# First cross-attention of a two-layer decoder: context loaded in the stage before, chunks split beside the maxima, stacks filled from SBUF

## The reference

```python
def _L0_xattn_ref(q, k, v, mask, wq, bq, wk, bk, wv, bv, wo, bo):
    H, D_K = 16, 16                        # context k = v: 2 x 1024 x 256
    qh = _split_heads(q @ wq.T + bq, B)
    kh = _split_heads(k @ wk.T + bk, B)
    vh = _split_heads(v @ wv.T + bv, B)
    scores = jnp.einsum('bhqd,bhkd->bhqk', qh, kh) / math.sqrt(D_K)
    scores = jnp.where(mask == 0, jnp.float32(-1000000000.0), scores)
    out = jnp.einsum('bhqk,bhkd->bhqd', softmax(scores), vh)
    return out.transpose(0, 2, 1, 3).reshape(B, -1, D_MODEL) @ wo.T + bo
```

## Time and profile before

| what | us |
|---|---|
| median of 3 runs | 1187.73 |
| lowest, highest | 1184.6, 1197.11 |
| the profiled execution, its own time | 1187.39 |
| its span, first to last instruction | 1185.6 |
| first cross stage, first SP issue to the next stage's | 144.3 to 448.7 |
| its first score | 218.07 |
| hard cross stage, first instruction | 815.6 |

### The profile page before, as it was taken

The page is one execution under the profiler, slowest core; times in us unless marked ns, Lnnn a source line. Parts: engine busy times, 40 slices in busy tenths (PEclk is TensorE's granted clock), DMA queues, the critical chain, the costliest instruction groups (busy, mean ns, idle before and its releaser), DMA issues. The chain is left out here.

```text
span 1185.6 us, 13004 instructions
## 1 busy us (share of the span) xinstructions
PE 943.2 (80%) x4000; PEld 472.9 (40%) x4005; DVE 668.0 (56%) x1347; ACT 455.2 (38%) x900; POOL 307.0 (26%) x294
## 2 busy tenths in 40 slices
PE   6879677699999985996489999894958888636985
PEld 3435434123333245664345555453412223412554
DVE  5845585698999633121354445444667885323534
ACT  3775132067777740111143233321206666202321
POOL 7144654000000002001254444454210000065014
PEclk9989988589999996799699999997968999858998
DMA  6000047434535005112540000000321110342000
GB/s 197 1 1 1 18 143 187 115 89 120 151 104 165 6 1 199 50 61 63 205 180 1 1 1 1 1 0 23 73 48 46 39 40 1 137 157 83 27 9 27
DMA packets 45279, 82.13 MB, mean 69 GB/s; under 512 B 9881, under 2 KB 31433, under 8 KB 43273
## 3 DMA queue, kind: packets, MB, share of 16 engines
q1 hardware_dynamic: 42081, 75.55, 21.2%
q0 software_dynamic: 2176, 5.38, 1.3%
q10 hardware_dynamic: 960, 0.43, 0.1%
HBM read 60.08 MB, written 16.54 MB: 65 GB/s over the span
## 5 line engine op out<-in xcount | busy, mean ns | idle before, releaser
L1050 DVE TENSOR_REDUCE c_amx<-PS 128x1 f32<-128x512 f32 x256 | 158.4, 682 | 28.3 <-PE PS L961 28.0
L1141 ACT ACTIVATE c_aE<-PS 128x512 f32<-128x512 f32 x256 | 132.6, 603 | 44.8 <-PE PS L973 44.5
L1599 POOL TENSOR_SCALAR s_Pn<-s_Pr,s_rs 128x512 f32<-128x512 f32 x64 | 99.9, 1563 | 123.0 <-DVE s_rs L1626 122.8
L961 PE MATMUL PS<-c_aKs,c_aQs 99*128 99x512 bf16 x256 | 106.5, 419 | 19.5 <-DMA c_aQs<-c_q_stack 18.6
L67 POOL TENSOR_SCALAR rstd<-mv 128x4 f32<-128x4 f32 x10 | 2.3, 232 | 388.0 <-DVE mv L90 387.3
L1617 DVE TENSOR_REDUCE s_mx<-PS 128x1 f32<-128x512 f32 x64 | 44.2, 691 | 100.3 <-PE PS L1730 100.3
L973 PE MATMUL PS<-c_aQs,c_aKs 99*128 99x512 bf16 x256 | 95.8, 385 | 3.4 <-ACT c_aE L1141 2.3
L1683 ACT ACTIVATE s_Pr<-PS,s_nmx 128x512 f32<-128x512 f32 x64 | 44.0, 687 | 137.4 <-DVE s_nmx L1619 137.4
L1050 DVE TENSOR_REDUCE h_amx<-PS 128x1 f32<-128x512 f32 x128 | 79.8, 684 | 26.7 <-PE PS L961 26.5
L1748 PE MATMUL PS<-s_PT,s_V 128*128 128x512 f32 x128 | 67.1, 606 | 18.6 <-DVE s_PT L1633 18.2
L1141 ACT ACTIVATE h_aE<-PS 128x512 f32<-128x512 f32 x128 | 66.9, 603 | 33.5 <-PE PS L973 33.3
(11 more groups left out here) (372 smaller groups left out, 1718.2 us busy)
## 6 DMA issues: line engine op xcount, KB each, us to landing
area<-in_e_w SPq DMA_DIRECT2D x16, 512.0 KB, 9.1
area<-in_g_w SPq DMA_DIRECT2D x8, 1024.0 KB, 17.0
c_aVs<-c_VB SPq DMA_DIRECT2D x8, 512.0 KB, 16.5
g_B<-in_g_b SPq DMA_DIRECT2D x1, 4096.0 KB, 11.6
c_k_stack<-area SPq DMA_DIRECT2D x12, 256.0 KB, 4.6
c_aKs<-c_k_stack SPq DMA_DIRECT2D x8, 384.0 KB
area<-in_ctxT SPq DMA_DIRECT2D x2, 1024.0 KB, 10.0
c_q_stack<-area SPq DMA_DIRECT2D x16, 128.0 KB, 2.5
```

Source lines behind the costliest of these rows:

```text
L961: pe.matmul(PS[:, n % MB, :], self.Qs[u % 3][:, j, qt * P:(qt + 1) * P], self.Ks[u % 3][:, j % self.KH, half * BANK:(half + 1) * BANK], st ...
L1050: dve.tensor_reduce(self.mx[:, qt, j, half:half + 1], PS[:, n % MB, :], AX.X, ALU.max).then_inc(self.max_done, 1)
L1141: act.activation(self.E[kt % 2][:, j, :], PS[:, MB + x % XB, :], ACT.Exp, scale=0.25).then_inc(self.exp_done, 1)
L1599: pool.tensor_scalar(Pn[g % NPB][:, :], Pr[g % NPB][:, :], rs[:, g % NPB:g % NPB + 1], None, ALU.mult).then_inc(pn_ready, 1)
```

## The change

- **Early loads.** A new area `early` (8488 words a partition, released after the cross stage) holds mixer buffers and, once these are used up, key weights, context, mask, and the other small inputs of the cross stage (`EarlyKeys`). SP loads them in the mixer after the last gate tile has been read (ScalarE L642, the last of them started at 62.65 us). VectorE converts the mask in the mixer, before its last output. TensorE computes key chunks 0 and 1 at the mixer's end.
- **First unit first.** Only key chunks 0 and 1 and query chunk 0 (`near`) are split before the attention. VectorE makes their residuals and third parts. The other nine chunks (`far`), value tiles 0 to 7 and the product of value bias and output weights come beside the maxima of unit 0, in `prologue`, one chunk or two tiles after each group of four scores. Their first residual and third part are made by GpSimd, their first and second parts by ScalarE. Value tiles 8 to 15 come in units 0 to 3, two in each (`during`, kt = 3 on TensorE, kt = 4 on ScalarE).
- **Fill from SBUF.** The DRAM stacks of the cross stage go. SP fills each block of 16 rows of a stack by one DMA from 64 rows of a part (6 for keys, 6 for queries, of 128 and 64 KB), and two for the tails. Those of unit 0 are issued part by part as these become ready.
- **Values** are read by TensorE from VB directly, 17 columns wide instead of 32; no load into Vs, in both cross stages.
- **Value bias** goes through the output weights into the output bias instead of being added to each value tile.
- **Tails.** The query tail comes from DRAM as an input, in the hard stage also the key tail; GpSimd's operations for them go, in both stages. The key tail of the cross stage is made by ScalarE.
- **Expert weights** of the next stage are all loaded after the last unit's fill.

The diff, cut:

```diff
-AREA = 17160
+AREA = 16384
+EARLY = 8488
...
+    XC = [early.take([P, B, PAD + S]) for n in range(2)]
+    CV = [early.take([P, B, S]) for n in range(2)]
+    w_in = early.take([P, KD, 2 * DI + 2 * DS + HEADS])
+    keys = sh.keys
...
+            sp_.wait_ge(silu_ready, len(convs))
+            sp_.wait_ge(proj_taken, 2 * len(convs) + NT)
+            keys.load(sp_)
...
+            keys.mask_vector(dve)
...
+            pe.wait_ge(st_ready, states_before(NT))
+            pe.wait_ge(t1_ready, carried_before(NT))
+            keys.first_chunks(pe)
...
-VW = 32
+VW = HD + 1
+MW = 32
...
-                pe.wait_ge(self.v_loaded[u % 3], (u // 3 + 1) * 16)
+                self.wait_values(pe, u // NG)
                 if u > 0:
                     pe.wait_ge(self.o_copied, u)
             pe.wait_ge(self.exp_done, (u * KT + kt + 1) * GH)
             for j in range(GH):
-                last = pe.matmul(PS[32 * j:32 * j + 32, 6, :], self.Vs[u % 3][:, kt, j % self.KH, :],
+                last = pe.matmul(PS[32 * j:32 * j + VW, 6, :], self.V[:, u, kt, j % self.KH, :],
...
+                    if before_maxima:
+                        before_maxima(pe, u)
...
+                if during:
+                    during(pe, u, kt)
...
+            if prologue:
+                prologue(pe, c)
...
-        sp.dma_start(at.Vs[buf][:, :, :, :],
-                     values[:, bass.ds(u, 1), :, :, :].rearrange("p u t h c -> p (u t) h c")).then_inc(at.v_loaded[buf], 16)
...
+    RING = (6, 5, 3, 4, 7)
+    FIRST = 2
...
+    def load(self, sp):
+        A, NK = self.A, self.NK
+        sp.dma_start(self.wk[:, :, :], A["c_wk"]).then_inc(self.wk_in, 16)
+        sp.dma_start(self.ctxT[:, :, 0:NK], A["ctxT"][:, :, 0:NK]).then_inc(self.ctx_in[0], 16)
+        sp.dma_start(self.maski, A["mask"].unsqueeze(0).to_broadcast([P, B, NK])).then_inc(self.mask_in, 16)
+        for d, name in ((self.wq, "c_wq"), (self.wv, "c_wv"), (self.bq, "c_bq"), (self.bk, "c_bk"), (self.ktc, "c_ktc")):
+            sp.dma_start(d[tuple(slice(None) for _ in d.shape)], A[name]).then_inc(self.rest_in, 16)
+        sp.dma_start(self.ctxT[:, :, NK:2 * NK], A["ctxT"][:, :, NK:2 * NK]).then_inc(self.ctx_in[1], 16)
+    def mask_vector(self, dve):
+        dve.wait_ge(self.mask_in, 16)
+        dve.tensor_scalar(self.mask[:, :, :], self.maski, 0.0, None, ALU.not_equal).then_inc(self.masked, 1)
+    def chunk(self, pe, n, bank):
+        b, m, half = n // 4, n // 2 % 2, n % 2
+        c0 = b * self.NK + half * BANK
+        for k in range(KD):
+            last = pe.matmul(bank, self.wk[:, k, m * P:(m + 1) * P], self.ctxT[:, k, c0:c0 + BANK],
+                             start=(k == 0), stop=(k == KD - 1))
+        last.then_inc(self.mm, 1)
+    def first_chunks(self, pe):
+        pe.wait_ge(self.wk_in, 16)
+        pe.wait_ge(self.ctx_in[0], 16)
+        for n in range(self.FIRST):
+            self.chunk(pe, n, self.PS[:, self.RING[n], :])
+KEY_SLOTS = ((0, 3, 5), (1, 4), (2,))
+QUERY_SLOTS = ((0, 1, 2), (3, 4), (5,))
...
+    made = [("k", 0), ("k", 1), ("k", 2), ("k", 3), ("q", 0), ("k", 4), ("k", 5), ("q", 1), ("q", 2), ("k", 6), ("k", 7),
+            ("q", 3)] + [("v", t) for t in range(KT)] + [("bo", 0)]
+    taken_by_scalar = [("q", 1), ("q", 2), ("q", 3)] + [("v", t) for t in range(KT)] + [("bo", 0)]
+    taken_by_scalar += [("v", t) for t in range(KT, NV)]
+    near = [("k", 0), ("k", 1), ("q", 0)]
+    far = [("k", 2), ("k", 3), ("k", 4), ("k", 5), ("q", 1), ("q", 2), ("k", 6), ("k", 7), ("q", 3)]
...
+            def tails(u):
+                sp.dma_start(at.Qs[u % 3][TAIL:ROWS, :, :].rearrange("r h n -> r (h n)").bitcast(U16),
+                             A["q_tail"]).then_inc(at.loaded[u % 3], 16)
+                sp.wait_ge(tails_set, u // NG + 1)
+                sp.dma_start(at.Ks[u % 3][TAIL:ROWS, :, :], ktail[:, u // NG, :].unsqueeze(1)
+                             .to_broadcast([TAIL_ROWS, GH, NK])).then_inc(at.loaded[u % 3], 16)
+            def key_part(u, p):
+                b, g = divmod(u, NG)
+                src = KP[p][g % 2 * 64:g % 2 * 64 + 64, b, g // 2, :]
+                for slot in KEY_SLOTS[p]:
+                    sp.dma_start(at.Ks[u % 3][slot * HD:(slot + 1) * HD, :, :], src).then_inc(at.loaded[u % 3], 16)
+            def query_part(u, p):
+                b, g = divmod(u, NG)
+                src = QP[p][g % 2 * 64:g % 2 * 64 + 64, g // 2, b * S:(b + 1) * S]
+                for slot in QUERY_SLOTS[p]:
+                    sp.dma_start(at.Qs[u % 3][slot * HD:(slot + 1) * HD, :, :], src).then_inc(at.loaded[u % 3], 16)
+            def load(u, buf):
+                if u >= 2:
+                    pair = [("k", 2 * (u // 2)), ("k", 2 * (u // 2) + 1), ("q", u // 2)]
+                    sp.wait_ge(far_p2_ready, 1 + max(far.index(c) for c in pair))
+                    tails(u)
+                for p in range(3):
+                    if u == 0:
+                        sp.wait_ge((p0_ready, p1_ready, p2_ready)[p], 2)
+                    key_part(u, p)
+                    if u == 0:
+                        sp.wait_ge((p0_ready, p1_ready, p2_ready)[p], len(near))
+                    query_part(u, p)
+            for u in range(2):
+                tails(u)
             sp.dma_start(wo[:, :, :], A["c_wo"]).then_inc(wo_in, 16)
             sp.dma_start(bo[:, :], A["c_bo"]).then_inc(wo_in, 16)
+            sp.dma_start(bvc[:, :, :], A["c_bv"]).then_inc(wo_in, 16)
+            at.sync(sp, load, lambda: None)
+            for n in range(3):
+                sp.wait_ge(at.loaded[n], 16 * loads * len(range(n, UNITS, 3)))
+            sp.wait_ge(xb_ready, 1)
+            for e in range(ExpertWeights.EXP):
+                sh.weights[0].load_expert(sp, e)
...
+            pool.memset(VB[:, :, :, :, HD:VW], 1.0).then_inc(v_ones, 1)
+            def last_part(i):
+                pool.wait_ge(p1_ready, len(near) + i + 1)
+                pool.tensor_tensor(part(*far[i], 2), R[i % 4], part(*far[i], 1), ALU.subtract).then_inc(far_p2_ready, 1)
+            for i, c in enumerate(far):
+                pool.wait_ge(p0_ready, len(near) + i + 1)
+                if i >= 4:
+                    pool.wait_ge(far_p2_ready, i - 3)
+                pool.tensor_tensor(R[i % 4], F[i % 4], part(*c, 0), ALU.subtract).then_inc(far_r_ready, 1)
+                if i > 0:
+                    last_part(i - 1)
+            last_part(len(far) - 1)
...
+            normalise(0)
+            dve.wait_ge(keys.rest_in, 80)
+            for n in range(2):
+                take_keys(n, FK[n])
+            normalise(1)
+            for n in range(2):
+                dve.wait_ge(p0_ready, n + 1)
+                dve.tensor_tensor(RK[n], FK[n], part("k", n, 0), ALU.subtract).then_inc(r_ready, 1)
+            at.set_ones(dve)
+            dve.wait_ge(p0_ready, 3)
+            dve.scalar_tensor_tensor(out=RQ, in0=bank("q", 0), scalar=bq[:, 0:1], in1=part("q", 0, 0), op0=ALU.add,
+                                     op1=ALU.subtract).then_inc(q0_taken, 1)
+            for i, (c, r) in enumerate(zip(near, RK + [RQ])):
+                dve.wait_ge(p1_ready, i + 1)
+                dve.tensor_tensor(part(*c, 2), r, part(*c, 1), ALU.subtract).then_inc(p2_ready, 1)
+            for n in range(2, 5):
+                take_far_keys(n)
+            def prologue(dve, c):
+                for n in {0: (5,), 2: (6,), 3: (7,)}.get(c, ()):
+                    take_far_keys(n)
+            at.vector(dve, meanwhile=lambda: projection.vector(dve, 0), prologue=prologue)
...
+            take_transposed(0)
+            for n in range(2):
+                act.wait_ge(k_taken, n + 1)
+                first_part(("k", n), FK[n])
+            act.wait_ge(r_ready, 1)
+            act.activation(part("k", 0, 1), RK[0], ACT.Copy).then_inc(p1_ready, 1)
+            act.wait_ge(q_mm, 1)
+            act.activation(part("q", 0, 0), bank("q", 0), ACT.Identity, bias=bq[:, 0:1]).then_inc(p0_ready, 1)
+            act.wait_ge(r_ready, 2)
+            act.activation(part("k", 1, 1), RK[1], ACT.Copy).then_inc(p1_ready, 1)
+            act.wait_ge(q0_taken, 1)
+            act.activation(part("q", 0, 1), RQ, ACT.Copy).then_inc(p1_ready, 1)
+            take_transposed(1)
+            for i in range(4):
+                far_first(i)
+                if i > 0:
+                    far_second(i - 1)
+            take_queries(1)
+            far_first(4)
+            far_second(3)
+            take_queries(2)
+            far_first(5)
+            far_second(4)
+            far_first(6)
+            far_second(5)
+            take_queries(3)
+            for t in (0, 1):
+                take_values(t)
+            far_first(7)
+            far_second(6)
+            for t in (2, 3):
+                take_values(t)
+            far_first(8)
+            far_second(7)
+            for t in (4, 5):
+                take_values(t)
+            far_second(8)
+            for t in (6, 7):
```

(55 more changed lines are left out.)

402 lines of the change are left out of this document (200 added, 202 removed).

## The result

The changed kernel takes 1136.5 us (median of 4 runs, 1131.7 to 1139.7) against 1187.5 (4 runs): a ratio of 0.955, 95% interval 0.949 to 0.962. Forecast were 1137 and a range of 1126 to 1162. The profiled execution took 1139.7 us, 3 above its median, so single stages are compared by marks counted from their own start, and not by the span.

What follows compares the result with a forecast made beforehand. In the first cross stage, a serial preparation with no engine full, then VectorE's maxima, then a TensorE-bound unit loop. -58.6 + 5.3 + 1.3 + 8 - 6.8 = -50.8 from 1187.4 gives 1136.6, said as 1137 us; range 1126 to 1162.

Steps and rivals of the forecast that it cites:

- Start of the stage: First cross stage: early loads and mask conversion cost nothing; two early key chunks delay its start 0.7 us, to 145.0.
- First score: First cross stage's preparation: shorter chain and fill bring the first score at 159.5 instead of 218.1, 58.6 us gained.
- Beside the maxima: Unit 0 of the first cross stage: added chunks and value tiles stretch the maxima from 19.9 to 25.2, 5.3 us lost.
- rival A: Beside unit 0's maxima TensorE stays at half clock, groups take 47 us instead of 25: 1159 us; chance 0.10.
- Unit loop: First cross stage, units 0 to 3: two value tiles each cost 2.0 us a unit, 8 us lost (7.2 to 12.2).
- Hard stage: Start of the hard cross stage: without GpSimd's tail operations normalisation is shorter, 6.8 us gained (5 to 7.9).
- B: First cross stage: POOL's subtraction chain ends the preparation, 8 us later if delayed, TensorE waits 5: 1142 us; chance 0.08.
- C: First cross stage's fills: 16 partitions run at 22 GB/s, 54 us a unit: 1391 us; decides from 50 GB/s; chance 0.03.
- D: First cross stage's first fill: keeps to 60 GB/s, 20 us, first score at 170.5: 1148 us; chance 0.09.
- E: Before the first cross stage: early loads don't hide, context lands 10 us after issue: 1147 us; chance 0.02.

Runs made afterwards that it cites:

- the repeats: The changed kernel run again with nothing changed: 1140.0 us (ratio 0.957) and, beside two other versions on one chip, 1137.1 us (ratio 0.958).

## Why the prediction was right

The view that carried it was the windows by stage: a preparation in which no engine is full gives back what is taken from its chain, and a TensorE-bound loop charges what is put in.

- **Start of the stage.** Allowed 0.7 us for the two early chunks; the stage's first work follows GpSimd's last statistic by 1.7 us instead of 1.3, so 0.4. The early loads and the mask cost the mixer nothing that stands out of its 5 us of scatter, which the runs put down to the clock.
- **First score.** Forecast 14.5 us after the start, measured 16.1. The engines were ahead of the sum: the third parts stood 9.6 us after the start (reckoned 10.5), since at the full clock a batch's transposes took 1.04 us and not 1.7. The fill was behind it: 6.5 us from there to the score instead of 4.0. This term was mis-sized, and its issues most of all: the last one ended 3.1 us behind the third parts, where I had put it 0.4 behind them, and its landing took 3.4 where I had left 3.6. I took 172 GB/s and 0.37 us an issue from rows of loads from DRAM into 19 to 48 partitions; fills from SBUF into 16 partitions cost 0.6 us an issue and moved 158 GB/s before the score, 124 to 129 where the whole fill was issued at once. Faster issues brought 0.5 and 0.7 us, so both limits lie close together. By the page "SBUF — State Buffer" of the Trainium skill, section "Door 1: The DMA port swizzle", my estimate was 109 GB/s and 3 us more; the trace has 158 GB/s and 1.6 us, between that and my value, and no run here went as low as 109.
- **What the gain is made of.** Undone singly, the tail operations cost 9.3 us at the first score, the early part 16.3, the order 26.5 (21.2 net of what goes beside the maxima). These overlap, and each has a loss of clock or of fill rate in it that the undoing brings with it (2.5 us of the 9.3 for the tails), so their sum, 52 beside 57.6 us, is not a split of the gain. What the filling from SBUF gives in itself, against a way through DRAM, was not tried in the first stage; in the hard one it is 9.0, together with the query stack's earlier load.
- **Beside the maxima.** +6.5 for +5.3. The groups took 3.1 us each, as reckoned (2.48 + 0.63). The 1.2 us on top fit the dip of the clock behind the wait for the fill, rival A in small: where the clock was at 0.50 and then 0.73 to 0.82 in the first 8 us, this stretch took 27.0 to 27.1 us in three profiles, where it was at 0.57 to 0.75 and then 0.82 to 1.00, 26.05 to 26.44 in five. The kernel after never had it at 1.00 there.
- **Unit loop.** +8 forecast, 7.2 for the tiles themselves, the lower bound: ScalarE's copies are free. The whole rest of the stage lost only 4.8 to 6.2 in three profiles of after. The loop without the tiles took 166.3 us from first to last negated maxima against 167.4 before: 1.1 of the difference. Another 1.1 already stands in the table's row for the first transposed score, since that longer way lies inside the first interval of negated maxima. That leaves 7.2 - 1.1 - 1.1 = 5.0. Why the loop itself is 1.1 us shorter was not tried. The later fills held nothing up: TensorE waited for no DMA in the loop. The expert weights moved at 347 to 366 GB/s from 330 to 350 us, twice the rate I had reckoned, and were in well before 398.9.
- **Hard stage.** -6.8 forecast, -7.1 at the mark. The rest of that stage took 134.6 us in the first profile against 131.1 before, but 130.7 to 134.6 over the profiles of kernels that share it, so this was no cost.
- **The rivals.** A held for the first 4 us only (0.68, then 0.89 in the next four and 1.00 later; in the repeats 0.57 and 0.50, then 1.00 and 0.82); behind 15.5 idle us, with all chunks first, it held for the whole stretch. B did not show: the maxima's transposes, which wait for the last chunk too, were released by the copy of the bias, 0.5 us late. GpSimd's last third part ended at 181.7, before the negated maxima. C and D had the right place and too low a rate: 124 GB/s, the lowest seen while a fill was waited for, stands far above the 50 from which C decides and the 60 of D. E was real as a mechanism, 16 us, but the loads did hide.

Misses of 1.7 and 1.2 us in the preparation and of 3.2 in the loop, which has 0.8 of it in the term that I had named, cancelled in part. That forecast and median lie 0.5 us apart is luck beyond this.
